# Layernorms behind three 16-head cross-attentions: a separate stage, or inside the attention's loop

## The reference

```
def _layernorm(x, axis=-1, eps=1e-05):
    m = jnp.mean(x, axis=axis, keepdims=True)
    v = jnp.var(x, axis=axis, keepdims=True)
    return (x - m) / jnp.sqrt(v + eps)
...
x = x + _L0_xattn_ref(_layernorm(x), ctx_1024, ctx_1024, ...)
x = x + _L0_attn_ref(_layernorm(x), gamma, beta, Wqkv, Wout)   # linear attention
...
x = x + _L2_xattn_ref(_layernorm(x), ctx_1024, ctx_1024)       # no weights
x = x + _L2_attn_ref(_layernorm(x), ...)                       # softmax attention, rms norm per head
...
x = x + _L3_xattn_ref(_layernorm(x), ctx_1024, ctx_1024, mask, ...)
x = x + _L3_attn_ref(_layernorm(x), ...)                       # gated recurrence
```

## Time and profile before

| | us |
|---|---|
| median of 3 runs | 2846.32 (2844.6 to 2846.47) |
| the profiled execution, its own time | 2843.08 |
| its span, first to last instruction | 2841.2 |
| TensorE busy | 2468.6 (87%) |
| VectorE busy | 1713.5 (60%) |
| ScalarE busy | 1398.4 (49%) |
| GpSimd busy | 665.1 (23%) |

### The profile page before, as it was taken

The page is one execution under the profiler, slowest core; times in us unless marked ns, Lnnn a source line. Parts: engine busy times, 40 slices in busy tenths (PEclk is TensorE's granted clock), DMA queues, the critical chain, the costliest instruction groups (busy, mean ns, idle before and its releaser), DMA issues. The chain is left out here.

```text
span 2841.2 us, 83215 instructions
## 1 busy us (share of the span) xinstructions
PE 2468.6 (87%) x35827; PEld 2089.7 (74%) x35827; DVE 1713.5 (60%) x3397; ACT 1398.4 (49%) x3496; POOL 665.1 (23%) x862
## 2 busy tenths in 40 slices
PE   6999787999958999999997759977996766999888
PEld 5888555777746999999996548976775645999567
DVE  5777675666656433333324755657885776777663
ACT  3888424555532444444432324426884554777342
POOL 3111002212102300000000203432336535555200
PEclk9999898999988999999999859987999898999999
DMA  2110003212031100000000042332321001211100
GB/s 76 39 36 21 17 0 96 62 33 62 3 85 49 33 17 17 17 17 17 2 2 24 3 144 85 139 109 80 98 66 52 2 2 49 55 51 45 45 1 30
DMA packets 118221, 126.66 MB, mean 45 GB/s; under 512 B 10877, under 2 KB 110152, under 8 KB 117864
## 3 DMA queue, kind: packets, MB, share of 16 engines
q1 hardware_dynamic: 114024, 110.93, 12.7%
q0 software_dynamic: 3840, 10.49, 1.2%
HBM read 105.67 MB, written 15.73 MB: 43 GB/s over the span
## 5 line engine op out<-in xcount | busy, mean ns | idle before, releaser
L1030 ACT ACTIVATE s_ca_probs<-s_ca_scores,s_ca_neg_max 128x256 f32<-128x256 f32 x768 | 352.8, 477 | 35.0 <-DVE s_ca_neg_max L1074 25.5
L1074 DVE TENSOR_REDUCE s_ca_neg_max<-s_ca_scores 128x4 f32<-128x1024 f32 x192 | 234.3, 1221 | 54.5 <-PE s_ca_scores L936 27.0
L953 PE MATMUL s_ca_probs_flipped<-identity,s_ca_probs 128*128 128x128 f32 x1536 | 214.2, 284 | 11.4 <-ACT s_ca_probs L1030 10.4
L2064 DVE COPY s_mx_w_mixed<-s_mx_ps 128x512 f32<-128x512 f32 x256 | 163.7, 684 | 95.0 <-PE s_mx_ps L1910 81.5
L953 PEld LDWEIGHTS s_ca_probs_flipped<-identity,s_ca_probs 128*128 128x128 f32 x1536 | 168.1, 143 | 50.1 <-ACT s_ca_probs L1030 23.1
L2019 ACT COPY s_mx_w_mixed<-s_mx_ps 128x512 f32<-128x512 f32 x256 | 137.3, 589 | 108.1 <-PE s_mx_ps L1897 86.1
L620 PE MATMUL s_ln_flip<-identity,s_ln_xn 128*128 128x128 f32 x352 | 66.4, 372 | 108.4 <-DVE s_ln_xn L602 108.3
L1030 ACT ACTIVATION_READ_ACCUMULATOR s_ca_probs<-s_ca_scores,s_ca_neg_max 128x1 f32 x768 | 160.2, 209 | 0.0
L1037 ACT COPY s_ca_probsT<-s_ca_probs_flipped 128x512 f32<-128x512 f32 x192 | 115.1, 599 | 80.1 <-PE s_ca_probs_flipped L953 80.1
L857 POOL TENSOR_TENSOR s_ca_inv_spread<-s_ca_inv_sums,h_ca_own_half 128x128 f32<-128x128 f32 x192 | 72.6, 399 | 343.1 <-DVE s_ca_inv_sums L1096 343.1
L82 PE MATMUL s_cc_shared<-s_cc_ctxT_low,h_cc_wkv_high 128*128 128x256 f32 x512 | 146.2, 286 | 2.2 <-DVE s_cc_ctxT_low L1425 2.2
(11 more groups left out here) (513 smaller groups left out, 7374.5 us busy)
## 6 DMA issues: line engine op xcount, KB each, us to landing
h_ca_ctxT<-in_ctxT SPq DMA_DIRECT2D x96, 256.0 KB, 3.1
h_mx_w_by_input<-in_L_ffn_eW1T SPq DMA_DIRECT2D x16, 512.0 KB, 5.5
h_mx_w_by_hidden<-in_L_ffn_eW2T SPq DMA_DIRECT2D x8, 1024.0 KB
h_re_win<-in_L_ffn_W_in SPq DMA_DIRECT2D x8, 1024.0 KB, 5.9
h_ca_ctx<-in_ctx SPq DMA_DIRECT2D x32, 256.0 KB, 2.8
x_normed_transposed<-in_ctx SPq DMA_DIRECT2D x7, 1024.0 KB, 5.7
h_re_wout<-in_L_ffn_W_out SPq DMA_DIRECT2D x8, 512.0 KB, 3.9
choice_results<-s_rt_zeros SPq DMA_DIRECT2D x4, 1024.0 KB, 10.5
```

The lines of the kernel that those rows point to most:

```text
L953: last = nc.tensor.transpose(psT[u % len(psT)][:, 2 * a + c, :], PR[b % 2][:, 4 * n + 2 * h + a, c * P:(c + 1) * P], ident[:, :])
L1030: last = nc.scalar.activation(PR[b % 2][:, p, :], psS[:, p // 2, (p % 2) * NKEY:(p % 2 + 1) * NKEY], ACT.Exp, bias=nmax[b % 2][:, p:p + 1] ...
L1074: nc.vector.tensor_reduce(nmax[b % 2][:, 4 * n:4 * n + 4], psS[:, 2 * n:2 * n + 2, :].rearrange("p r (g k) -> p r g k", g=GR), AX_X, ALU.m ...
L2064: last = nc.vector.tensor_copy(part(int(name[1]), r), bank(j, r))
```

## The change

Three of the layernorm stages go: those behind X0, X2 and X3. Their work is done by a new helper, `GroupNorm`, spread over the cross-attention's loop. VectorE aggregates each tile's mean and variance in `statistics`; at every fourth tile (batches 8, 16, 24 and the end) it works out a first guess of the inverse root by integer operations on the bits, and three Newton steps of four operations, for the four tiles at once (`guess`, `refine`). GpSimd scales the rows, a pair of tiles at a time (`normalise`; with `residual` it scales `X` too), at the end of its work for batches 10, 12, 18, 20, 26 and 28. TensorE transposes the pair into the attention's output bank `psO` in the next batch (11, 13, 19, 21, 27, 29) behind the first half of the probabilities' transposes, having waited for the readers of that bank, and waits before attending until ScalarE has stored the pair. The pairs 6 and 7 (last four tiles) are left to the next stage: VectorE refines their roots at its start, and scaling, transposes and stores stand between the first steps there.

The next stages' weights are loaded in the cross-attention, ahead of its own loads on SP, and the split of the head weights follows GpSimd's work of batches 0 and 1. Semaphores of `held` are now cleared with those of the stages and no longer at the very end.

```diff
-    def prepare(self, pool):
+    def prepare(self, pool, c):
         pool.wait_ge(self.s_wq, 16)
-        for c in range(KC):
-            pool.tensor_copy(self.WH[:, c, :], self.W[:, c, :]).then_inc(self.s_wh, 1)
-            pool.wait_ge(self.s_wh, c + 1)
-            pool.tensor_tensor(self.WL[:, c, :], self.W[:, c, :], self.WH[:, c, :].bitcast(F32), ALU.subtract).then_inc(self.s_wl, 1)
+        pool.tensor_copy(self.WH[:, c, :], self.W[:, c, :]).then_inc(self.s_wh, 1)
+        pool.wait_ge(self.s_wh, c + 1)
+        pool.tensor_tensor(self.WL[:, c, :], self.W[:, c, :], self.WH[:, c, :].bitcast(F32), ALU.subtract).then_inc(self.s_wl, 1)
...
+class GroupNorm:
+
+    GROUP = 4
+    MAGIC = 0x5f3759df - 0x400000
+    STEPS = 3
+
+    def __init__(self, sb, sem, X, XNT, ident, ST, twice=False, affine=None, residual=False):
+        self.X, self.XNT, self.ident, self.ST = X, XNT, ident, ST
...
+    def load(self, sp):
+        if self.affine:
+            for n, v in enumerate(self.affine):
+                sp.dma_start(self.col[:, n, :], v).then_inc(self.s_col, 16)
+
+    def statistics(self, dve, i):
+        dve.bn_stats(self.ST[:, i, :], self.X[:, i, :]).then_inc(self.s_st, 1)
+        dve.wait_ge(self.s_st, i + 1)
+        dve.bn_aggr(self.MV[:, i, :], self.ST[:, i, :]).then_inc(self.s_mv, 1)
+
+    def guess(self, dve, g):
+        n, t = self.roots, slice(g * self.GROUP, (g + 1) * self.GROUP)
+        half, bits, root = self.half[:, t, :], self.bits[:, t, :], self.root[:, t, :]
+        link = Chain(dve, self.s_dve, g * (n + 1))
+        dve.wait_ge(self.s_mv, (g + 1) * self.GROUP)
+        link(dve.tensor_scalar(half[:, :, 0], self.MV[:, t, 1], 0.5, 0.5 * EPS, ALU.mult, ALU.add))
+        if n == 2:
+            link(dve.tensor_scalar(half[:, :, 1], self.MV[:, t, 1], 0.5 * (1.0 + EPS), 0.5 * EPS * EPS, ALU.mult, ALU.add))
+        link(dve.tensor_scalar(bits, half.bitcast(I32), 1, None, ALU.logical_shift_right))
+        dve.tensor_scalar(root.bitcast(I32), bits, -1.0, float(self.MAGIC), ALU.mult, ALU.add).then_inc(self.s_guess, 1)
+
+    def refine(self, dve, g):
+        t = slice(g * self.GROUP, (g + 1) * self.GROUP)
+        half, root, step, mean = self.half[:, t, :], self.root[:, t, :], self.step[:, t, :], self.MV[:, t, 0]
+        shift, gain, back = self.shift[:, t], self.gain[:, t], self.back[:, t]
+        link = Chain(dve, self.s_newton, g * (4 * self.STEPS + 1 + self.residual))
+        dve.wait_ge(self.s_guess, g + 1)
+        for _ in range(self.STEPS):
+            link(dve.tensor_tensor(step, root, root, ALU.mult))
+            link(dve.tensor_tensor(step, step, half, ALU.mult))
+            link(dve.tensor_scalar(step, step, -1.0, 1.5, ALU.mult, ALU.add))
+            link(dve.tensor_tensor(root, root, step, ALU.mult))
+        if self.residual:
+            dve.tensor_scalar(gain, root[:, :, 0], 1.0, 1.0, ALU.mult, ALU.add)
+            link(dve.tensor_tensor(back, mean, root[:, :, 0], ALU.mult))
+            dve.tensor_scalar(back, back, -1.0, 0.0, ALU.mult, ALU.add)
+        link(dve.tensor_tensor(shift, mean, root[:, :, self.roots - 1], ALU.mult))
+        dve.tensor_scalar(shift, shift, -1.0, 0.0, ALU.mult, ALU.add).then_inc(self.s_scale, 1)
+
+    def normalise(self, pool, u):
+        pool.wait_ge(self.s_scale, 2 * u // self.GROUP + 1)
+        if u:
+            pool.wait_ge(self.s_f, u)
+        for k in range(2):
+            i = 2 * u + k
+            last = pool.tensor_scalar(self.XN[:, k, :], self.X[:, i, :], self.root[:, i, self.roots - 1:self.roots], self.shift[:, i:i + 1],
+                                      ALU.mult, ALU.add)
+        last.then_inc(self.s_n, 1)
+        if self.residual:
+            pool.wait_ge(self.s_n, u + 1)
+            for k in range(2):
+                i = 2 * u + k
+                last = pool.tensor_scalar(self.X[:, i, :], self.X[:, i, :], self.gain[:, i:i + 1], self.back[:, i:i + 1], ALU.mult, ALU.add)
+            last.then_inc(self.s_back, 1)
+
+    def flip(self, pe, u, dst):
+        dst = dst.rearrange("p (c k n) -> p c k n", c=KC, k=2)
+        pe.wait_ge(self.s_n, u + 1)
+        for k in range(2):
+            for c in range(KC):
+                last = pe.transpose(dst[:, c, k, :], self.XN[:, k, c * P:(c + 1) * P], self.ident[:, :])
+        last.then_inc(self.s_f, 1)
+
+    def store(self, act, u, src):
+        cols = slice(2 * u * P, (2 * u + 2) * P)
+        src = src.rearrange("p (c n) -> p c n", c=KC)
+        act.wait_ge(self.s_f, u + 1)
+        if self.affine:
+            act.wait_ge(self.s_col, 32)
+            for c in range(KC):
+                last = act.activation(self.XNT[:, c, cols], src[:, c, :], ACT.Identity, bias=self.col[:, 1, c:c + 1], scale=self.col[:, 0, c:c + 1])
+        else:
+            last = act.copy(self.XNT[:, :, cols], src)
+        last.then_inc(self.s_out, 1)
...
-def cross_attention(nc, X, ST, QT, ident, ones, held, mask=None):
+def cross_attention(nc, X, ST, QT, ident, ones, held, norm, mask=None, loads=(), ahead=None):
...
+        NORM = {b: 2 * ((b - 9) // 8) + (b % 8 == 5) for b in range(9, NB) if b % 8 in (3, 5)}
...
+                for weights in loads:
+                    weights.load(sp)
+                norm.load(sp)
                 for b in range(NB):
                     load(b)
...
                             pool.wait_ge(s_o, b + 1)
                             held.values(pool, b + 2)
+                    if ahead and b < KC:
+                        ahead(pool, b)
+                    if b + 1 in NORM:
+                        norm.normalise(pool, NORM[b + 1])
...
                     flip(b, 0)
+                    if b in NORM:
+                        pe.wait_ge(s_at, b)
+                        pe.wait_ge(s_we, (b - 1) // 2)
+                        norm.flip(pe, NORM[b], psO[:, :])
                     if OWN and b + 2 < NB:
                         project_keys(b + 2)
...
+                    if b in NORM:
+                        pe.wait_ge(norm.s_out, NORM[b] + 1)
                     attend(b)
                 finish(TILES - 1)
...
                     turned(b, 0)
+                    if b in NORM:
+                        norm.store(act, NORM[b], psO[:, :])
                     if OWN and b + 2 < NB:
                         keys(b + 2)
...
-                    nc.vector.bn_stats(ST[:, i, :], X[:, i, :])
+                    norm.statistics(dve, i)
+                    if i % 4 == 3:
+                        norm.guess(dve, i // 4)
+                    if i % 4 == 3 and i < TILES - 1:
+                        norm.refine(dve, i // 4)
...
                 nc.gpsimd.memset(VS[:, :, P:P + 1], 1.0).then_inc(s_one, 1)
+                for u in (6, 7):
+                    norm.normalise(pool, u)
...
                 attend(0)
+                norm.flip(pe, 6, psN[:, :])
                 body(1, 0)
+                pe.wait_ge(norm.s_out, 7)
+                norm.flip(pe, 7, psN[:, :])
                 with pe.Fori(2, LAST) as i:
...
-                with act.Fori(1, LAST - 1) as i:
+                norm.store(act, 6, psN[:, :])
+                result(0)
+                take(3)
+                exponentiate(2)
+                norm.store(act, 7, psN[:, :])
+                act.wait_ge(norm.s_out, 8)
+                with act.Fori(2, LAST - 1) as i:
...
+                norm.refine(dve, 3)
                 dve.wait_ge(s_w, 64)
                 key_features(0)
                 query_features(0)
                 body(0)
+                dve.wait_ge(norm.s_back, TILES // 2)
                 with dve.Fori(1, LAST) as i:
...
                 low(2)
+                norm.normalise(pool, 6)
                 pool.wait_ge(softmax.s_w, 48)
                 for t in range(TILES):
                     normalise(t)
+                    if t == 1:
+                        norm.normalise(pool, 7)
                     if t + 3 < TILES:
                         low(t + 3)
...
                     if t < TILES:
                         project(t)
+                    if t in (LAG, LAG + 2):
+                        u = 6 + (t - LAG) // 2
+                        norm.flip(pe, u, psN[u % 2][:, :])
                     if t >= LAG:
                         flip(t - LAG)
...
+                    if t in (LAG, LAG + 2):
+                        u = 6 + (t - LAG) // 2
+                        norm.store(act, u, psN[u % 2][:, :])
+                        act.wait_ge(norm.s_out, u + 1)
                     if t >= LAG:
...
                 project(0, 0)
                 project(0, 1)
+                for u in (6, 7):
+                    norm.flip(pe, u, psG[u % 2][:, :])
+                pe.wait_ge(norm.s_out, 8)
                 for t in range(NT):
...
                     update_gate(0, m)
+                for u in (6, 7):
+                    norm.store(act, u, psG[u % 2][:, :])
                 for t in range(NT):
...
-        if "L0x" in STAGES:
+        with held(nc, kept) as (sb, sem):
```

(14 more changed lines are left out.)

87 lines of the change are left out of this document (49 added, 38 removed).

## The result

The changed kernel takes 2886.8 us (median of 4 runs, 2883.7 to 2889.3) against 2846.4 us: a ratio of 1.0131, 95% interval 1.0116 to 1.0147. It is slower, by 40 us; 2879 was forecast, 2842 to 2905 the range. The profiled executions are 2885.8 and 2841.2 us long (spans): 44.6 us to account for.

A forecast was written before the change was run, and what follows sets the result against it. TensorE was taken as nearly always busy in the three cross-attentions, VectorE and ScalarE close behind in X2. 2843.1 - 35.6 + 28.2 + 3.0 + 14.7 + 8.5 + 8.0 + 6.0 = 2875.9, as median 2879 us; range 2842 to 2905.

The forecast's parts named there:

- removed: Three layernorm stages behind X0, X2 and X3: of their 40.55 us, 35.6 go.
- (a): Root bursts on VectorE at every eighth batch of the loops stall TensorE: 28.2 us added, from 0 to 34.2.
- (b): Aggregations outside bursts: hidden in X0 and X3, passed in part to ScalarE in X2, 3 of 3.6 us.
- (c): Flips, six a loop: extra transposes, and in X2 a wait for GpSimd's scaling; 14.7 us, from 8.3 to 20.
- (d): Next-stage weights on SP delay X3's first mask and so the first attention: 8.5 us, from 0 to 10.
- (e): Next stages take over leftover work: linear attention 0.7, per-head normalisation 4.0, recurrence 3.3; sum 8.0 us, from 3 to 14.
- (f): TensorE's clock falls behind six of nine bursts in the loops, 1 us each: 6.0 us, from 0 to 30.
- The first rival: In the loops, buffers hide the bursts, so the kernel is faster: 2831 us, chance 0.14.
- the second: Half of bursts, flips, loads and next-stage costs is hidden, no change: 2844 us, chance 0.06.
- the clock's rival: Clock falls at every burst and X2 stays low for long, 30 us for 6: 2903 us, chance 0.17.
- the fourth rival: GpSimd slows VectorE's small burst operations, 0.06 us more each on average, 10 us: 2889 us, chance 0.13.
- the tail work only fills the gap that it leaves: Last four tiles' work, moved into the next stages, fills the freed gap: 14 instead of 8.0 us, 2885.

The follow-up runs named there:

- filled2: Changed kernel plus idle identity transposes on TensorE where each of the nine bursts leaves it waiting; 2881.6 us against 2853.2 for the kernel before, ratio 1.0105.
- second pair: Second profiles of the unmodified changed kernel and of the kernel before; single executions of 2877.8 and 2845.9 us.
- x2_order: Changed kernel, only in X2: GpSimd scales the two tiles ahead of its attention wait and values' copy, not behind them; ratio 1.0120.
- nh_late: Changed kernel, only in the per-head normalisation behind X2: the last four tiles' scaling, flips and stores five positions later; ratio 1.0148.
- lean: Changed kernel with bursts in place but roots in fewer dependent operations; 2858.2 us against 2838.9 for the kernel before, ratio 1.0060.
- spread2: Changed kernel with each group's guess and refine in four pieces behind the inverse sums of batches 9 to 12 of the eight; ratio 1.0066.

## Why the prediction was right, and what was wrong in it

The steps against what was measured, in the first pair of profiles; bursts and flips by filled2, the clock as the difference to it:

```
step                          predicted   measured
removed                         -35.6      -35.5
(a) bursts: X0, X2, X3           28.2       27.3   (10.3, 9.2, 7.8; predicted 10.05, 9.9, 8.25)
(b) aggregations in X2            3.0        0
(c) flips: X0, X2, X3            14.7       18.2   (3.3, 10.1, 4.9; predicted 3.3, 8.1, 3.3)
(d) loads in X3                   8.5        8.9   (7.4 in the second pair)
(e) next stages                   8.0        7.2   (-1.7, 7.4, 1.5; predicted 0.7, 4.0, 3.3)
(f) clock in the loops            6.0       17.5   (9.7 in the second profile)
stages with the same code         0          1.0   (with a clearing of semaphores, 1.4, that moved behind the recurrence taken as theirs)
sum                              32.8       44.6
```

The sum was forecast 12 us too low for this pair and hit by the second (31.9), in which the clock cost less. The median's 40 us lie between. So the closeness of 2879 to 2887 is in part luck of the clock; the direction and the terms (a), (c) and (d) are not.

- *The removed part and (a)* hold by size and, in X0 and X3, by cause: the hole stands where the prediction put it, ended by the copy, and its length follows the burst one to one. In X2 the price is right to 0.2 us a burst, but TensorE's hole is ended by GpSimd's spreading of the inverse sums; the prediction spoke of the exponentials. The first rival (buffers hide it) is refuted with a margin: the burst, shortened by 1.6 us, gave back all 1.6. With it falls the second, which hid half of everything. Without the clock X0, X2 and the whole of X3 grew by 13.6, 19.3 and 21.5 us, where 13, 21 and 20 were forecast.
- *(b)* was wrong. X2's tiles without a burst take 11.45 us with the aggregation and 11.44 without. A VectorE busy 81% of the time still had 0.2 us at that place.
- *(c)* named the right cause in X2, GpSimd's copy ahead of the scaling, with 1.0 us of wait; x2_order took 1.17 away a flip. What I subtracted there (0.2 us to spare) was not to be had, and in X3 a flip costs 0.5 to 0.9, not 0.55.
- *(d)* is right to 0.4 us: the small mask waited for the large weights, 13.1 us where about 12 was forecast. It did not overtake them.
- *(e)* is right in sum by luck. From X0's last addition to the start of the stage behind the linear attention 1.7 us more went than the gap accounts for (the table load of 1.28 us is gone there, as forecast), and behind X2 the price is almost twice the forecast, and for another reason: not GpSimd's order (nh_late) but its memsets, which held two of the refine's operations; in lean, where they hold none, 5.4 of the 7.4 us are gone.
- *(f)* is the term that was mis-sized: 6.0 us against 17.5 and 9.7 in two profiles. The prediction gave the clock's rival 30 us for 2903; the result lies between the two, 8 us above the forecast. Rows of the kernel before showed low stretches of 4 and 12 busy us behind such gaps; I took 1 us a burst for six of nine. In the first profile all nine intervals are longer than filled2's, by 0.9 to 3.2 us.
- *GpSimd beside VectorE's small operations*, the fourth rival: inside the bursts it is absent; they keep their 0.20 us. It is there where the two engines meet: behind X2, and in spread2's pieces. The prediction spread the 4.15 us of L602 evenly, 0.26 us each, and that reading was wrong. The durations (shortest, median, longest, in ns) and GpSimd's row say that a few instructions were held and the others not touched:

```profile
L602 DVE TENSOR_SCALAR s_ln_xn<-x_resident,s_ln_mean,s_ln_rstd x16: 398/410/1967, 2133.9 to 2142.9; 128x256 f32<-128x256 f32 x16
2136.99 1.80 POOL L417 TENSOR_TENSOR h_nh_w_low<-h_nh_w,h_nh_w_high 128x768 fp32r<-128x768 f32 x1
```

Four of the sixteen took 0.91 to 1.97 us, each beside one of GpSimd's four instructions. Read so, the cost is that of a meeting, not a tax on each operation. In the stage behind X2 the memsets held a TENSOR_SCALAR for 4.82 us, while TENSOR_TENSOR took 0.16 beside the same memsets, and 0.60 to 0.65 beside GpSimd's subtraction. The Trainium skill, "GPSIMD Engine Reference", section "Key points", names two cases of contention, a two-port mode and two SBUF inputs. The trace agrees for operations with two inputs in SBUF beside GpSimd's subtraction, and not beside its memsets; that the held TENSOR_SCALAR is the two-port case would fit, but no run here shows an operation's mode.

That the tail work only fills the gap that it leaves is refuted too: 35.5 us went and 7.2 came back.

What stays open: why the clock falls behind some holes and not behind others of the same loop (X0, 3.2 us: one of three in the second profile, three in the first; lean: one of 1.37 us and none of 2.17), and what makes the stages with the same code differ by several us from one execution to the next. The flips in X3, which cost more behind a high clock (0.9 and 0.7) than behind the low one (0.5 and 0.7), are only measured, and so is the part of X2's 3.1 us a burst that lies outside TensorE's hole of 2.18.
